# Weighted edge sweeps: edge network on two partition halves, bias seeded by ScalarE, scatter sums beside the weights of the block three ahead

## The reference

```python
h = jax.nn.relu(edge_feat @ W1 + b1)                 # 32 -> 64; last layer: 8 -> 64 -> 64, silu
w = (h @ W2 + b2).reshape(e, 4, MUL, MUL)            # 256 weights an edge
m0 = ALPHA * (einsum('ei,eio->eo', s_e * sh0[:, None], w_000)
              + C110 * einsum('eim,em,eio->eo', v_e, sh1, w_110))
m1 = ALPHA * (einsum('ei,em,eio->eom', s_e, sh1, w_011)
              + einsum('eim,eio->eom', v_e * sh0[:, None, None], w_101))
out0 = segment_sum(m0, dst, num_segments=n)
out1 = segment_sum(m1.reshape(e, MUL * 3), dst, num_segments=n)
```

## Time and profile before

| | us |
|---|---|
| median of 3 runs | 19001.58 (18997.28 to 19043.8) |
| span of the profiled execution | 18741.8 |
| first sweep, first to last window add | 5348.2 |
| last sweep, first to last window add | 5435.9 |
| PE busy | 14220.5 (76%) |
| DVE busy | 12292.2 (66%) |
| POOL busy | 9141.7 (49%) |
| ACT busy | 5069.6 (27%) |

### The profile page before, as it was taken

How to read it: one execution, slowest core, us unless ns; L and a number is a source line. 1 busy time by engine, 2 the same in 40 slices (tenths; PEclk the granted TensorE clock), 3 DMA queues, 4 the chain that set the end, 5 groups by cost and what they waited for, 6 DMA issues and landing times. The chain is left out here.

```text
span 18741.8 us, 308593 instructions
## 1 busy us (share of the span) xinstructions
PE 14220.5 (76%) x89407; PEld 10314.7 (55%) x89407; DVE 12292.2 (66%) x24385; ACT 5069.6 (27%) x12977; POOL 9141.7 (49%) x9516
## 2 busy tenths in 40 slices
PE   6877777777766666666666689899778888888887
PEld 4554555555546666656565667676444444444444
DVE  6666766666665565655565558578666666666666
ACT  1111111111123333333333357476211111111112
POOL 4555555555545555555555400100455555555554
PEclk7777777777765555555555569789788887888887
DMA  1111111111111111111111056365011111111111
...
DMA packets 1106496, 699.39 MB, mean 37 GB/s; under 512 B 853332, under 2 KB 1021953, under 8 KB 1105890
## 3 DMA queue, kind: packets, MB, share of 16 engines
...
## 5 line engine op out<-in xcount | busy, mean ns | idle before, releaser
L598 PE MATMUL weighted_weights_ps<-weighted_w_out,weighted_hidden 128*128 128x256 f32 x12600 | 4494.0, 490 | 6.3 <-DVE weighted_to_s L723 3.2
L428 POOL DMA_INDIRECT weighted_rows<-x_after_convolved,weighted_idx x3140 | 3054.3, 973 | 2483.1 <-DMA weighted_sh<-in_sh 1568.6
L428 POOL DMA_INDIRECT weighted_rows<-in_x,weighted_idx x3140 | 3026.6, 964 | 2398.9 <-DMA weighted_sh<-in_sh 1471.6
L859 POOL DMA_INDIRECT coupled_rows<-x_after_weighted,coupled_idx x3125 | 2956.2, 946 | 2206.2 <-DMA coupled_sh<-in_sh 1230.5
L598 PEld LDWEIGHTS weighted_weights_ps<-weighted_w_out,weighted_hidden 128*128 128x128 f32 x12600 | 2641.7, 232 | 2262.4 <-issue 1957.5
L870 PE MATMUL coupled_win<-coupled_onehot,coupled_prod 128*125 128x64 f32 x12500 | 2602.4, 398 | 892.1 <-issue 554.9
L870 PEld LDWEIGHTS coupled_win<-coupled_onehot,coupled_prod 128*125 128x125 f32 x12500 | 2528.1, 312 | 943.4 <-issue 584.1
L588 PE MATMUL weighted_hid_ps<-weighted_feat,weighted_w_in 32*64 32x320 f32 (+1 forms) x3786 | 1754.3, 549 | 1256.1 <-ACT weighted_hidden L647 791.0
L631 PEld LDWEIGHTS weighted_win_ps<-weighted_onehot,weighted_prod 128*128 128x128 f32 x12560 | 1945.5, 226 | 121.8
L718 DVE TENSOR_TENSOR weighted_v_v<-weighted_weights_ps,weighted_scaled 128x320 f32<-128x320 f32 x3768 | 1957.3, 574 | 0.0
L647 ACT ACTIVATE weighted_hidden<-weighted_hid_ps,weighted_b_in 64x320 f32<-64x320 f32 x1262 | 659.6, 523 | 4728.0 <-remote 2067.5
...
## 6 DMA issues: line engine op xcount, KB each, us to landing
...
```

Of the source, the lines that this page charges most:

```text
L428: pool.indirect_dma_start(rows[s][:, t, :], None, table, bass.IndirectOffsetOnAxis(ap=idx[s][:, t:t + 1].bitcast(U32), axis=0))\
L598: mm = pe.matmul(banks[bank][:, t * WPATHS:(t + 1) * WPATHS], hidden[slot][:, t * P:(t + 1) * P], w_out[:, :], start=True, stop=True)
L859: pool.indirect_dma_start(rows[s][:, t, :], None, table, bass.IndirectOffsetOnAxis(ap=idx[s][:, t:t + 1].bitcast(U32), axis=0))\
```

## The change

The diff touches `weighted_edges`, its constants and the layout of one input.

- The first layer runs once a block. The edge features of the two halves lie one below the other, `w_in` holds the matrix twice on its diagonal (64x128), and one matmul of 320 columns gives the hidden units of 320 edges on partitions 0 to 63 and those of the other 320 on 64 to 127. The deep network's middle matrix is laid out likewise (128x128). Two PSUM banks, `hid_ps[0]` and `hid_ps[1]`, are used in turn by block, in the deep network by layer.
- The weights are six matmuls that contract 64 rows, on alternating partition halves (`TURN_OF`): four of 128 edges, and the middle tile as two of 64 edges.
- The bias of the weights is no longer a row of ones. ScalarE copies a tile `seeds` (1280 columns of bias, 64 of zeros) into the bank group (`seed`), when VectorE has released it. The matmuls add to it, without a start flag. Six matmuls ahead of the loop write the banks once so that additions take effect.
- The scatter sum of block n is written into 64 more columns of the bank group of block n+3, behind its weights, and one semaphore tells VectorE of both. `BEHIND` is 3 instead of 1. VectorE adds it ahead of the last read of the bank. The adds behind the loop are gone, since the three padding blocks carry them.
- TensorE and ScalarE run the first layer one block further ahead (n+4).

Core of the diff:

```diff
-BEHIND = 1
+BEHIND = 3
-        hidden = ring("hidden", [P, BLOCK])
+        hidden = ring("hidden", [P, HALF])
-        hid_ps = psum("hid", [P, 512])
-        win_ps = psum("win", [P, 512])
+        hid_ps = [psum("hid0", [P, 512]), psum("hid1", [P, 512])]
...
+                    m = b * PER_BLOCK + u
+                    if deep and u == 1:
+                        hold(pe, hidden_ready, m, held)
+                    elif not isinstance(b, int) or m >= 2:
+                        hold(pe, hidden_ready, m - 1, held)
+                    to = hid_ps[u if deep else slot % 2]
...
+                TURN_OF = ((0, 0, 0), (3, 1, P // 2), (1, 0, P), (4, 1, P + P // 2))
+
+                def weight_mm(b, slot, bank):
+                    pe.wait_ge(hidden_ready, (b + 1) * PER_BLOCK)
+                    pe.wait_ge(seeded, b + 1)
+                    for t, h, at in TURN_OF:
+                        rows = slice(h * HID, (h + 1) * HID)
+                        pe.matmul(banks[bank][:, t * WPATHS:(t + 1) * WPATHS], hidden[slot][rows, at:at + P],
+                                  w_out[rows, :], start=False, stop=True, skip_group_check=True)
+                    for h, at in ((0, 2 * P), (1, 0)):
+                        rows = slice(h * HID, (h + 1) * HID)
+                        mm = pe.matmul(banks[bank][rows, 2 * WPATHS:3 * WPATHS], hidden[slot][rows, at:at + HID],
+                                       w_out[rows, :], start=False, stop=True, skip_group_check=True)
+                    return mm
+
+                def scatter(b, slot, bank):
+                    pe.wait_ge(msg_ready, b + 1)
+                    for t in range(TILES):
+                        mm = pe.matmul(banks[bank][0:MSG, WIN_AT:WIN_AT + WINDOW], prod[slot][:, t, :],
+                                       onehot[slot][:, t, :], start=False, stop=True, skip_group_check=True)
+                    return mm
...
-                            both(n + 3, (s + 3) % SLOTS, g + (s + 3) // SLOTS, n + 2, (s + 2) % SLOTS, s % 2)
-                            pe.wait_ge(summed, n + p * BEHIND + 2)
-                            pe.wait_ge(msg_ready, n + 1)
+                            both(n + 4, s, g + 1, n + BEHIND, (s + BEHIND) % SLOTS, (s + BEHIND) % 2, s)
...
+                def seed(b, bank):
+
+
+                    act.wait_ge(w_used, b + 1)
+                    nc.scalar.activation(banks[bank][:, 0:WIN_AT + WINDOW], seeds[:, :], ACT.Copy).then_inc(seeded, 1)
...
+                        seed(g * SLOTS + s + BEHIND, (s + BEHIND) % 2)
+                        layers(g * SLOTS + s + SLOTS, s)
...
+                            add_window(n, banks[s % 2], bases[s])
                             dve.wait_ge(vec, n * VEC + 3)
                             dve.tensor_tensor(to_s[:, :, :, :], w_s,
                                               scaled[:, :, None, 0:2 * MUL].broadcast_to([P, TILES, MUL, 2 * MUL]),
                                               ALU.mult).then_inc(w_used, 1)
...
-                            add_window(n + 1, n + p * BEHIND, bases[s])
```

165 lines of the change are left out of this document (79 added, 86 removed).

## The result

The changed kernel takes 18870.2 us, median of 4 runs (18825.7 to 18887.8), against 19022.7 us (18997.3 to 19052.7) of the kernel before. The ratio is 0.9921, with a 95% interval of 0.9896 to 0.9947. The direction was right. The size was not: the forecast was 17070 us, and 18870 us lies above the range, which ended at 18450.

A forecast was written before the change was run, and what follows sets the result against it. Late TensorE ends, paid in full, were taken to bound the weighted sweeps. Blocks falling to 7.0 and 7.1 us gain 628 x (1.52 + 1.56) = 1930 us: 19001.6 - 1930 = 17070 us, range 16130 to 18450 us.

The forecast's parts named there:

- The floors: In the weighted sweeps, VectorE's work is 5.8 us a block and GpSimd's gathers 6.28 us, the floor of any version.
- TensorE's work: TensorE's sweep block after the change: 6.3 us at 1.2 GHz, 3.3 at 2.4 in the first; 7.5 and 4.0 in the second.
- rival C: Chance 0.12: the weight matmuls' row halves do not overlap, so their pairs run one after the other; 18450 us.
- The seed: ScalarE's copy of 1344 bias columns into the bank ahead of the weights takes 1.35 us, with 2.6 kept as alternative.
- The loop: The sweeps' chain of waits over two blocks swallows lateness of 5.7 us at 2.4 GHz and 3.3 us at 1.2 GHz.
- The clock: TensorE's 1.2 and 2.4 GHz levels in the sweeps: lateness beyond the slack was averaged over both, 1.1 us.
- Late ends: TensorE's ends reach ScalarE 4.2, 4.8, 6.5 us late, one block in two; beyond the slack this costs 0.7 us a block.
- the prediction's own formula: Two sweep blocks of time T last 6.8 us plus lateness L at 2.4 GHz, 9.2 us plus L at 1.2 GHz.
- its wait for `weighted_sh`: GpSimd's wait for the weighted_sh load was to be nearly gone in the profile after the change.
- D: Chance 0.04: the sweeps' stall moves but does not shrink, late ends growing until two blocks last as before; 18950 to 19060 us.
- E: Chance 0.11: slower, at the seed's wait; GpSimd never pauses while gathering, so every TensorE end is late; 19700 us.
- The last of the signs against me: Wrong if ScalarE or VectorE still wait over 2 us a block on TensorE ends that its rows show long past.

The follow-up runs named there:

- e10: Changed kernel with plain loads in place of the sweeps' gathers and three useless matmuls ahead of each first-layer matmul: 15252 us, ratio 0.817.
- e2: Changed kernel with the five gathers of each sweep block replaced by one plain SyncE load of the same bytes: 15873 us, ratio 0.846.
- e5: Kernel before the change with the five gathers of each sweep block replaced by one plain SyncE load of the same bytes: 15266 us, ratio 0.816.
- e11: Changed kernel with a GpSimd memset of 128 x 1024, waited for, behind each block's five gathers: 18177 us, ratio 0.973.
- e13: Changed kernel with useless matmuls ahead of each first-layer matmul and a GpSimd memset of 128 x 1024 behind each block's gathers: 18434 us, ratio 0.966.
- e4: Changed kernel with one scatter matmul of five in each block of the weighted sweeps: 18206 us, ratio 0.971.
- e14: Changed kernel, all gathers kept, with three useless matmuls (filler) ahead of each first-layer matmul and no rest for GpSimd: 19256 us, ratio 1.010.
- e17: Changed kernel with useless matmuls ahead of each first-layer matmul and a GpSimd memset of 128 x 32 behind each block's gathers: 18069 us, ratio 0.964.
- e16: Changed kernel with useless matmuls ahead of each first-layer matmul and a GpSimd memset of 128 x 512 behind each block's gathers: 17832 us, ratio 0.936.

## Why the prediction was right and wrong

Step by step:

- **The floors.** Right. With the gathers cut the sweep runs at VectorE's 5.77 us (5.8 foretold). The 6.28 us for GpSimd stand in the gathers' own rows, 0.95 and 0.30 us five times.
- **TensorE's work.** Right. The six weight matmuls take 2008.53 - 2005.48 = 3.05 us at 1.2 GHz and 2012.43 - 2010.78 = 1.65 us at 2.4 GHz (2.86 and 1.47 foretold, 5.44 if they ran one after the other). The halves do overlap, and rival C fell.
- **The seed.** Right, 1291 ns against 1350.
- **The loop.** Right as a sum: at full clock and without gathers nothing in it reaches 5.8 us a block (e10).
- **The clock.** Not asked at all. The sum took high and low level as equally frequent, as in the kernel before. But the change takes work from TensorE while the pace stays, and the granted clock fell to 0.59 and 0.60. It ate the saving in the last sweep (TensorE busy 4426 us before and 4398 after). Without gathers that costs 0.9 us a block (e2 against e5); with gathers and rests little, since in e11 and e13 the clock is 0.57 and 0.77 in the first sweep, 0.56 and 0.83 in the last, and the pace the same. For TensorE's 7.5 us of the last sweep at 1.2 GHz the sum had 0.1 us. At a clock of 0.60, four fifths of the time at the low level, they alone would ask for an estimated 0.8 x 7.5 + 0.2 x 6.28 = 7.3 us a block, by the prediction's own figures and before any late end; e2's 6.85 us at 0.73 is much this term by itself (0.54 x 7.5 + 0.46 x 5.8 = 6.7).
- **Late ends: the step that failed.** The three ends that I read became a price of 0.7 us a block: a fixed disturbance, mostly swallowed by the slack that the new loop over two blocks gives. By the prediction's own formula, 2T = 6.8 + L at the high level and 9.2 + L at the low, the 8.39 us of the first sweep need L = 10.0 and 7.6 us, not 4.2 to 6.5. Lateness is not fixed: it grows with the time for which GpSimd has gathered without a rest. More slack lets GpSimd run on longer, and the ends come later by nearly as much. What sets the pace is that GpSimd must stop, and without a rest written into the program it stops when its four slots are full, because everyone waits for TensorE. That fits its wait for `weighted_sh` (3040.2 us in the whole program before, 3037.4 after), which I had foretold as nearly gone.

| sweep and kernel | mean run of gathers, us | waits on late ends, ScalarE, VectorE, us | us a block |
|---|---|---|---|
| first, 1000 to 5000 us: before | 10.4 | 1552.9, 702.9 | 8.53 |
| changed | 15.3 | 1453.8, 1135.7 | 8.41 |
| e4 one scatter | 18.3 | 1571.5, 1061.5 | 8.13 |
| last, 13600 to 18000 us: before | 9.3 | 1195.3, 542.8 | 8.67 |
| changed | 7.3 | 675.3, 406.8 | 8.64 |
| e4 one scatter | 11.0 | 1386.1, 941.9 | 8.14 |
| e14 filler alone | 12.4 | 1738.7, 1062.5 | 8.93 |

In the first sweep the runs grow as TensorE's work shrinks, which is the step that the prediction lacked. In the last sweep it is otherwise: the change did cut the late ends, from 1738 to 1082 us, and the pace stayed all the same, with the clock down from 0.82 to 0.60. Where filler lifts the clock to 0.80 again (e14), the runs and the late ends are back and above those of before. No run holds the clock up in the last sweep without more work on TensorE, so how the loss there is shared between clock and late ends stays open.

- **The rivals.** D, "the stall moves but does not shrink", at 0.04, names the outcome, though the time lies 80 us under its window: VectorE's idle time went from 3338 to 3386 us. E named the mechanism (ends are late because GpSimd never pauses) and took it to need the tail of what was seen. Both belonged together: E's mechanism limits itself at D's pace, since a pace faster than the gathers' rests allow brings the ends to a halt. The answer that came 2 us after the last gather in the earlier trace rows said it, and so did the 3.71 us ahead of the first gather in the earlier trace rows. I read those pauses as a surplus of GpSimd. They were what the ends needed.
- **What would show it.** The last of the signs against me, over 2 us a block of waits on ends long past, is what the profile shows: 1453.8 + 1135.7 us in 4000 us, some 475 blocks.

The gain of 0.8% is most likely what e4 shows in larger, a little less to do between late ends: by the sweeps' rows 112 us of the 152. The first sweep, where the saved work is the larger part, has 86 of them. This was argued, not tried.

Open is what a gather does to TensorE's signal. The runs show that it comes with GpSimd's issuing and not with the bytes (e2), nor with a busy GpSimd (e17, e16, e13), and that TensorE's own issue goes on meanwhile. Whether the matmul's last write or only its signal is held back, no row tells. It was not tried whether e16 needs its filler, nor the kernel before with the memset of 512; at the memsets of 1024 and 32 it was level with the changed kernel, so e16's gain is likely not owed to the change. Nor was a rest tried in the coupled stage, where in e2, without gathers in the sweeps, VectorE's window adds still wait 886.1 us on such ends.
